# Two expert feed-forward stages: the hidden product ahead of the low part, the down matmul three units behind, routing two blocks ahead in PSUM

## What is computed

```python
scores = sigmoid(x @ gate_w.T)                       # 32 experts
choice = scores + gate_bias
group_scores = top_k(choice in 4 groups of 8, 2).sum(-1)
masked = where(expert in the best 2 groups, choice, 0)
idx = top_k(masked, 8)
w = scores[idx] / (scores[idx].sum() + 1e-20) * 2.5
y = sum over experts of w * (silu(x @ Wg) * (x @ Wu)) @ Wd
y = y + (silu(x @ Sg) * (x @ Su)) @ Sd               # shared expert
```

## Time and profile before

| what | us |
|---|---|
| median of 3 runs | 2157.75 |
| lowest and highest | 2157.05, 2161.29 |
| profiled execution | 2158.21 |
| span of that execution, first to last instruction | 2156.4 |
| FFN1, first statistics to last addition | 273.7 to 617 |
| FFN2 | 1814.8 to 2156.4 |

### The profile page before, as it was taken

One profiled execution on the slowest core, in us unless ns is written; L12 is line 12 of the kernel. 1 busy time (PEld: TensorE's weight loads), 2 busy tenths in 40 slices (PEclk: granted clock), 3 DMA queues, 4 the chain that ended last, 5 costly groups with the idle time before them and its releaser, 6 DMA issues. The chain is left out here.

```text
span 2156.4 us, 54691 instructions
## 1 busy us (share of the span) xinstructions
PE 1953.6 (91%) x21984; PEld 1271.3 (59%) x21984; DVE 1836.4 (85%) x2705; ACT 1246.9 (58%) x2204; POOL 1476.6 (68%) x1044
## 2 busy tenths in 40 slices
PE   1799979999956999999999999999999997989998
PEld 1566653333324777777777777777777775533333
DVE  5577768888875999999999999999999997788886
ACT  2454445555534666666666666666666664555555
POOL 3100015555554999999999999999999995355555
PEclk9999969999967999999999999999999998899999
DMA  3222244665601000000000000000000000575565
GB/s 122 82 74 68 81 88 81 123 115 97 124 19 41 13 13 13 13 12 13 13 13 13 13 14 12 15 11 15 7 9 6 9 6 1 100 125 104 129 123 95
DMA packets 95452, 109.19 MB, mean 51 GB/s; under 512 B 31712, under 2 KB 56672, under 8 KB 94816
## 3 DMA queue, kind: packets, MB, share of 16 engines
q1 hardware_dynamic: 92368, 103.91, 22.6%
q10 hardware_dynamic: 2832, 1.79, 0.3%
HBM read 88.10 MB, written 17.57 MB: 49 GB/s over the span
## 5 line engine op out<-in xcount | busy, mean ns | idle before, releaser
L1111 POOL TENSOR_TENSOR ffn_sw<-ffn_sg,ffn_wide 128x512 f32<-128x512 f32 x256 | 324.9, 1269 | 556.3 <-ACT ffn_sg L1217 520.5
L938 DVE TENSOR_REDUCE head_shift<-head_score 128x64 bf16<-128x1024 f32 x512 | 624.3, 1219 | 83.4 <-PE head_score L750 71.6
L900 ACT ACTIVATE head_ex<-head_score 128x1024 f32<-128x1024 f32 x512 | 524.6, 1025 | 189.1 <-PE head_score L772 187.3
L707 POOL TENSOR_TENSOR head_half<-head_ex 128x1024 f32<-128x1024 f32 x256 | 604.9, 2363 | 27.1 <-ACT head_ex L900 27.1
L945 DVE TENSOR_TENSOR head_ex<-head_ex,head_recp 128x1536 f32<-128x1536 f32 x256 | 446.6, 1745 | 4.9 <-ACT head_recp L872 4.9
L782 PE MATMUL head_den<-head_half,c_ident 128*128 128x128 f32 x3072 | 385.3, 275 | 2.8 <-POOL head_half L708 2.7
L782 PEld LDWEIGHTS head_den<-head_half,c_ident 128*128 128x128 f32 x3072 | 363.1, 192 | 6.3 <-POOL head_half L708 3.2
L714 POOL TENSOR_TENSOR head_ex<-head_ex,head_recip 128x512 f32<-128x512 f32 x256 | 329.1, 1286 | 14.1 <-ACT head_recip L874 7.0
L772 PE MATMUL head_score<-head_shift,c_identb 128*128 128x512 bf16 x1024 | 309.0, 383 | 18.5 <-DVE head_shift L938 12.4
L750 PE MATMUL head_score<-att_b_HB,att_b_GR 96*128 96x256 f16 x2048 | 310.0, 273 | 11.5 <-DMA att_b_HB<-b_queries 10.9
L765 PE MATMUL head_outp<-head_ex,att_b_vs 128*32 128x128 f32 x8192 | 277.7, 277 | 0.0
(11 more groups left out here) (230 smaller groups left out, 2685.6 us busy)
## 6 DMA issues: line engine op xcount, KB each, us to landing
ffn_wide<-pair_weights SPq DMA_DIRECT2D x256, 256.0 KB, 9.5
a_keys<-band_parts_k SPq DMA_DIRECT2D x14, 295.5 KB, 2.5
att_a_HB<-a_keys SPq DMA_DIRECT2D x56, 73.9 KB
a_queries<-band_parts_q SPq DMA_DIRECT2D x14, 271.5 KB, 2.9
att_a_GR<-a_queries SPq DMA_DIRECT2D x14, 271.5 KB
b_queries<-head_parts_q SPq DMA_DIRECT2D x32, 96.0 KB, 1.6
att_b_HB<-b_queries SPq DMA_DIRECT2D x128, 24.0 KB
b_keys<-head_parts_k SPq DMA_DIRECT2D x24, 96.0 KB, 1.6
```

Of the source, the lines that this page charges most:

```text
L707: ch.link(pool.tensor_tensor(hf, e[:, 0:8, :], e[:, 8:16, :], ALU.add))
L900: act.activation(ex[:, kt % RING, :, h * QS:(h + 1) * QS], score[:, h, :, :].rearrange("p k (a w) -> p (k a) w", a=NH // 2), ACT.Exp, scal ...
L938: dve.tensor_reduce(shift[:, h, :], score[:, h, :, :].rearrange("p k (a w) -> p w k a", a=NH // 2), AX.XY, ALU.max, negate=True).then_inc( ...
L1111: pool.tensor_tensor(sw[:, unit % 2, :], sg[:, unit % 2, :], wide[:, k % 2, i, :], ALU.mult).then_inc(sw_ready, 1)
```

## The change

All of it is in `feed_forward`.

- DVE does the hidden product of a unit first and the low part of the unit before it second, then additions, routing and moments. ACT's order within a unit stays.
- `down_of` is called three units behind (LAG = 3) instead of two, and `h_parts` has three buffers. `take_down`, `turn_back` and `add_back` move by one unit.
- The routing has eleven pieces. Block 0 is still routed in the head; block 1 at units 0 to 7 and block 2 at units 9 to 16 of block 0; block k + 2 at units 5 to 15 of block k, for blocks 1 to 5. Blocks 6 and 7 have no routing. The weights of block 1 are turned at unit 9 of block 0, those of block k + 1 at unit 2 of block k.
- Most intermediate values of the routing lie in the PSUM bank `back`. `choice` is made for all blocks in the head. The values of a routing stay in `back` between the `add_back` of one block and the `turn_weights` of the next.
- The moments of a block are taken in halves, at unit 16 and at unit 0.
- In the head, `turned` uses four banks (the two of `hidden` and the two of `gate`), `normalise` is called two blocks ahead, and the weights of block 0 are turned after the logits of block 2.

The diff, cut to its core:

```diff
-    PIECES = 10
-    TURN_AT, STATS_AT = 13, 12
+    PIECES = 11
+    LAG = 3
+    STATS = {NU - 1: range(2), 0: range(2, TB)}
...
-        h_parts = m.sb("h_parts", [P, 2, 2, BLK], F16)
+        h_parts = m.sb("h_parts", [P, LAG, 2, BLK], F16)
...
+        def turned(k):
+            return (hidden, gate)[k // 2 % 2][:, k % 2, :]
+        def small(col, width):
+            return back[:, col:col + width]
...
+        def pieces_at(unit):
+            block, g = divmod(unit, NU)
+            if block == 0 and g < 8:
+                return 1, range(g * PIECES // 8, (g + 1) * PIECES // 8)
+            if block == 0 and g > 8:
+                return 2, range((g - 9) * PIECES // 8, (g - 8) * PIECES // 8)
+            if 0 < block < NBLK - 2 and 5 <= g < 5 + PIECES:
+                return block + 2, range(g - 5, g - 4)
+            return None, ()
...
# PE
-                if unit > 1:
-                    down_of(unit - 2)
-                if unit % NU == 2 and unit > NU:
+                if unit >= LAG:
+                    down_of(unit - LAG)
+                if turned_at(unit) is not None:
+                    turn_weights(turned_at(unit))
+                if unit % NU == LAG and unit > NU:
                     turn_back(unit // NU - 1)
-                if unit % NU == TURN_AT and unit // NU + 1 < NBLK:
-                    turn_weights(unit // NU + 1)
...
# DVE, routing: one input of each in PSUM
+            first, place, is_first = small(0, TB * EGRP), small(TB * EGRP, TB * EGRP), small(128, TB * NEXP)
+            ahead, group_copy = small(2 * TB * EGRP, TB * EGRP * EGRP), small(96, TB * EGRP)
+            rest, kept = small(256, TB * NEXP), small(384, TB * NEXP)
...
-                    L(dve.tensor_tensor(each(g2), each(g2), each(g1), ALU.add))
+                    L(dve.tensor_tensor(flat(second), flat(second), first, ALU.add))
...
+                    dve.tensor_tensor(flat(group), flat(second), first, ALU.add)
+                    L(dve.tensor_tensor(group_copy, flat(second), first, ALU.add))
...
# DVE, head
+                low_turned(k)
+                if k < NBLK - 2:
+                    normalise(k + 2)
+                if k > 0:
+                    choose(k - 1)
+                if k == 1:
                     for piece in range(PIECES):
                         route(0, piece)
...
# DVE, units
-            for unit in range(UNITS):
+            for unit in range(UNITS + 1):
+                if unit < UNITS:
+                    hidden_of(unit)
                 if unit > 0:
                     low_part(unit - 1)
-                hidden_of(unit)
-                if unit % NU == 3 and unit > NU:
+                if unit % NU == LAG + 1 and unit > NU:
                     add_back(unit // NU - 1)
```

More of the change, by code:

```diff
@@ L1028, in feed_forward @@
         xn, xs = m.sb("xn", [P, 2, TB, E]), m.sb("xs", [P, 2, BLK])
[L1029 to L1032 removed]
+        choice = m.sb("choice", [P, NT, NEXP])
+        masked, weights = m.sb("masked", [P, TB, NEXP]), m.sb("weights", [P, TB, NEXP])
+        second, group = m.sb("second", [P, TB, EGRP]), m.sb("group", [P, TB, EGRP])
+        better = m.sb("better", [P, TB, EGRP, EGRP])
         top, tot = m.sb("top", [P, TB, 8]), m.sb("tot", [P, TB])
@@ L1064, in weighed_before, with turned_at @@
             return unit // NU * NPAIR + max(unit % NU - 1, 0)
-        def route_piece(unit):
-            k, piece = unit // NU + 1, unit % NU
-            return (k, piece) if k < NBLK and piece < PIECES else (None, None)
+        def pieces_at(unit):
[7 more added lines that the diff above has]
+            return None, ()
+        def turned_at(unit):
+            block, g = divmod(unit, NU)
+            if block == 0:
+                return 1 if g == 9 else None
+            return block + 1 if g == LAG - 1 and block + 1 < NBLK else None
         @block.sync
@@ L1157, in down_of @@
                     pe.wait_ge(dT_ready, ONE + unit // NU)
-                product(pe, down[:, :], c["down_parts"], part_of(unit), h_parts[:, unit % 2, 0, :], h_parts[:, unit % 2, 1, :],
+                product(pe, down[:, :], c["down_parts"], part_of(unit), h_parts[:, unit % LAG, 0, :], h_parts[:, unit % LAG, 1, :],
                         start=(unit % NU == 0), stop=(unit % NU == NPAIR)).then_inc(down_done, 1)
@@ L1172, in _ @@
                     logits_of(k - 1)
-                if k == 2:
+                if k == 3:
                     turn_weights(0)
             logits_of(NBLK - 1)
-            pe.wait_ge(xlow_ready, ONE + NBLK + 1)
-            for unit in range(UNITS + 2):
+            pe.wait_ge(xlow_ready, ONE + NBLK)
+            pe.wait_ge(xs_ready, ONE + NBLK)
+            for unit in range(UNITS + LAG):
                 if unit < UNITS:
@@ L1240, in _ @@
                     high_part(unit - 1)
-                if unit % NU == 1 and unit > NU:
+                if unit % NU == LAG - 1 and unit > NU:
                     take_down(unit // NU - 1)
-                if unit % NU == TURN_AT and unit // NU + 1 < NBLK:
-                    take_weights(unit // NU + 1)
+                if turned_at(unit) is not None:
+                    take_weights(turned_at(unit))
             high_part(UNITS - 1)
@@ L1300, in best_experts, with choose @@
-            def best_experts(part):
-                if part == 0:
-                    L(dve.tensor_scalar(ta[:, :, :], ta[:, :, :], 0.0, None, ALU.add))
+                dve.tensor_tensor(xnT[:, 1, at], turned(k), xnT[:, 0, at], ALU.subtract).then_inc(xlow_ready, 1)
+            def choose(k):
+                dve.wait_ge(logits_read, ONE + k + 2)
+                at = slice(k * TB, (k + 1) * TB)
+                dve.tensor_tensor(choice[:, at, :], scores[:, at, :], c["gate_bias"][:, :][:, None, :].broadcast_to([P, TB, NEXP]),
+                                  ALU.add).then_inc(chosen, 1)
@@ L1304, in best_experts @@
+            def best_experts(k, piece):
+                if piece == 0:
+                    L(dve.scalar_tensor_tensor(groups(kept), member(place), TOPG - 0.5, groups(picked(k)), ALU.is_lt, ALU.mult))
+                    L(dve.tensor_scalar(masked[:, :, :].rearrange("p t e -> p (t e)"), kept, 0.0, None, ALU.add))
+                elif piece == 1:
                     for j in range(TB):
-                        last = dve.max(top[:, j, :], ta[:, j, :])
+                        last = dve.max(top[:, j, :], masked[:, j, :])
@@ L1336, in hidden_of, with route @@
+            def route(k, piece):
+                if piece < 6:
+                    best_groups(k, piece)
+                elif piece < 9:
+                    best_experts(k, piece - 6)
+                else:
+                    share(k, piece - 9)
             def hidden_of(unit):
```

164 lines of the change are left out of this document (79 added, 85 removed).

## The result

| kernel | median us | lowest and highest | runs | ratio to before, 95% interval |
|---|---|---|---|---|
| before | 2159.52 | 2157.05, 2161.31 | 4 | |
| changed | 2094.05 | 2091.78, 2094.95 | 4 | 0.9696, 0.9679 to 0.9713 |

What follows compares the result with a forecast made beforehand. PE was taken to bound quiet units, and long routing pieces on DVE that nothing covers the routed ones. Savings of 30.5 (FFN1), 27.6 (FFN2) and 2.7 us (heads), 60.8 in all, from 2157.75 gave 2097.0 us, range 2088 to 2116.

## What to carry to other kernels

When a short operation is long beside another engine's, read both timelines at that place: if it ends with the other engine's instruction, it lasts what that instruction has left to run (and 0.03 to 0.15 us more here), and moving the operation to later in the other's round can be worth as much as another memory (24.7 us against 21.3 here). Two cures of one loss don't add; price each with the other in place, and price what makes one of them possible. An engine that sits idle ahead of a short step behind a copy can be given the next unit's large step first, if the consumer is moved a unit further off as well.

## What was not expected of the hardware

An operation of DVE on 32 columns, one SBUF input and an output in SBUF, lasted 10.42 us beside two fills of POOL, of 3.51 and 7.35 us back to back: it did not get in between them, but waited for the end of the second. With its output in PSUM it takes 0.20 us beside the same fills, and the kernel is 10.9 us faster, the shorter normalisation included. The fills read nothing, and the operation has one SBUF input, so neither two SBUF inputs of DVE nor an input of POOL is needed for a hold-up. Within the routing, too, an operation with a single SBUF input was held up before the change, the masking in lines of the kernel before (shortest, median, longest):

```profile
L1303 DVE TENSOR_SCALAR ffn_ta<-ffn_ta x16: 227/576/691, 286.4 to 2091.9; 128x128 f32<-128x128 f32 x16
```

A reduction with its input in SBUF was not: it takes 0.28 us at 389.57, in the middle of the weighing from 388.85, in the kernel with values in SBUF. Nor was `MAX8`. The single-input operations that were held up in these traces are all `TENSOR_SCALAR` from SBUF to SBUF.
